# A two-layer decoder on one core: the first layer's decay sums loaded in halves, and its output store moved to the end of the store queue's step

## The reference

```
x = x + state_space(layernorm(x))            # m_ in the kernel
x = x + cross_attention(layernorm(x), ctx)   # c_
x = x + recurrent(layernorm(x))              # r_
```

```
decay = exp(A * dt_t)
state = state * decay + (x_t * dt_t) (outer) B_t
y_t   = state . C_t
y = (y + x * D) * silu(z);  y = y * rsqrt(mean(y*y) + eps) * norm_w
```

```
c = sigmoid(xt.wf + c.uf + bf) * c + sigmoid(xt.wi + c.ui + bi) * tanh(xt.wc + c.uc + bc)
h = tanh(x.wo + c_final.uo + bo)      # for every tile
```

## Time and profile before

| | us |
|---|---|
| median of 3 runs | 3414.84 |
| lowest and highest | 3406.63, 3415.68 |
| the profiled execution | 3411.43 |
| its span | 3409.5 |

### The profile page before, as it was taken

The page is one execution under the profiler, slowest core; times in us unless marked ns, Lnnn a source line. Parts: engine busy times, 40 slices in busy tenths (PEclk is TensorE's granted clock), DMA queues, the critical chain, the costliest instruction groups (busy, mean ns, idle before and its releaser), DMA issues. The chain is left out here.

```text
span 3409.5 us, 95859 instructions
## 1 busy us (share of the span) xinstructions
PE 3084.8 (90%) x27055; PEld 2664.0 (78%) x27056; DVE 2775.2 (81%) x8725; ACT 2260.3 (66%) x8248; POOL 1514.0 (44%) x5113
## 2 busy tenths in 40 slices
PE   6699999999999999999998699989898999499998
PEld 4578888888888888888886577777777777387998
DVE  5588888888888888888885588888888887687776
ACT  4467777777777777777775477777777777143333
POOL 1244444545444544445452155555555554133333
PEclk8789999999999999999999799999999999699999
DMA  6111111111111111111110200000000000023443
GB/s 190 37 36 50 44 41 41 41 48 47 41 41 41 42 47 46 41 41 41 48 48 14 61 20 15 18 15 18 17 17 18 15 19 13 4 103 121 131 136 90
DMA packets 123391, 161.87 MB, mean 47 GB/s; under 512 B 27331, under 2 KB 94832, under 8 KB 123312
## 3 DMA queue, kind: packets, MB, share of 16 engines
q1 hardware_dynamic: 111056, 126.37, 12.7%
q0 software_dynamic: 12256, 34.53, 2.8%
HBM read 102.85 MB, written 61.53 MB: 48 GB/s over the span
## 5 line engine op out<-in xcount | busy, mean ns | idle before, releaser
L380 POOL TENSOR_TENSOR tiny<-tiny 128x1 f32<-128x1 f32 x3456 | 776.0, 225 | 799.1 <-DVE tiny L367 558.3
L806 ACT ACTIVATE work<-bank,att 128x128 f32<-128x128 f32 x2048 | 722.0, 378 | 57.7 <-DVE att L796 51.8
L806 ACT ACTIVATION_READ_ACCUMULATOR work<-bank,att 128x1 f32 x2048 | 445.0, 217 | 0.0
L796 DVE TENSOR_REDUCE att<-bank 128x4 f32<-128x512 f32 x512 | 333.8, 683 | 47.1 <-PE bank L789 47.1
L825 PE MATMUL bank<-const,work 128*128 128x128 f32 x2048 | 318.1, 279 | 31.8 <-ACT work L806 26.1
L789 PEld LDWEIGHTS bank<-work 32*128 32x128 f32 x4096 | 254.0, 189 | 107.0 <-issue 74.7
L1286 DVE SCALAR_TENSOR_TENSOR work<-work,small 128x127 f32<-128x127 f32 (+2 forms) x1152 | 317.5, 345 | 16.0 <-ACT work L1126 10.7
L789 PE MATMUL bank<-work 32*128 32x128 f32 x4096 | 302.7, 286 | 21.1 <-ACT work L1171 2.5
L825 PEld LDWEIGHTS bank<-const,work 128*128 128x128 f32 x2048 | 239.5, 142 | 74.8 <-ACT work L806 58.7
L380 POOL TENSOR_TENSOR tiny<-tiny,const 128x1 f32<-128x1 f32 x1152 | 250.6, 218 | 90.3
L185 PE MATMUL bank<-w1r,workr 128*128 (+2 forms) x802 | 267.5, 333 | 0.5 <-issue 0.2
(11 more groups left out here) (357 smaller groups left out, 8472.8 us busy)
## 6 DMA issues: line engine op xcount, KB each, us to landing
work<-decay_sums SPq DMA_DIRECT2D x64, 512.0 KB, 3.7
work<-pair_rows SPq DMA_DIRECT2D x91, 258.0 KB
pair_rows<-extra SPq DMA_DIRECT2D x128, 182.0 KB
work<-in_ctx SPq DMA_DIRECT2D x128, 128.0 KB, 2.1
x_res<-in_x POOLq DMA_DIRECT2D x8, 1024.0 KB, 17.5
recurrence_out<-r_xo_ SPq DMA_DIRECT2D x64, 128.0 KB, 1.7
work<-recurrence_out SPq DMA_DIRECT2D x64, 128.0 KB
out_dram<-work POOLq DMA_INDIRECT x91, 2.5
```

What stands on the lines that cost most here:

```text
L380: e.tensor_tensor(out_, a_, b_, ALU.add if b_ is three_halves else ALU.mult)\
L796: e.tensor_reduce(a_nm[:, 4 * g:4 * g + 4], sc_banks[g % 2][:, :].rearrange("p (h k) -> p h k", k=P), AX.X, ALU.max, negate=True).then_inc ...
L806: last = e.activation(Pb[g % 2][:, c * P:c * P + P], sc_banks[g % 2][:, c * P:c * P + P], ACT.Exp, bias=a_nm[:, 4 * g + c:4 * g + c + 1], ...
```

## The change

The load of the decay sums becomes two loads of 2 KB per partition, for heads 0 to 3 and 4 to 7, each with a semaphore of its own (`m_cum0`, `m_cum1`). The first waits for the first half of the products of the tile before, the second for the second half. Neither waits for the square, which now writes into `m_zg_` (the gate, which at that point has been used). `m_relative` waits for its own half. In SyncE's step the order becomes: both loads, the context load, the blank stores, and last the output store, which is that of tile i-5 in place of i-4; the pipeline of SyncE runs one step further out.

```diff
-                def load_sums(b):
-
-                    if past(b): e.wait_ge(S["m_y"], 2 * b)
-                    if past(b): e.wait_ge(S["m_ss"], b)
+                def load_sums(b, half):
+
+                    if past(2 * b): e.wait_ge(S["m_y"], 2 * b - 1 + half)
                     src = cum_dram[b] if isinstance(b, int) else cum_dram[ds(b, 1)].rearrange("o n -> (o n)")
-                    e.dma_start(m_E.rearrange("p h t -> p (h t)"), src.partition_broadcast(P))\
-                        .then_inc(S["m_cum"], 16)
+                    at = slice(4 * P * half, 4 * P * half + 4 * P)
+                    e.dma_start(m_E.rearrange("p h t -> p (h t)")[:, at], src[at].partition_broadcast(P))\
+                        .then_inc(S[f"m_cum{half}"], 16)
...
                     if live(b):
-                        load_sums(b)
-                    b = i - 4
-                    if live(b):
-                        store_output(b)
+                        load_sums(b, 0)
+                        load_sums(b, 1)
                     b = i
                     if live(b):
                         load_context(b)
                     b = i
                     if live(b):
                         blank_rows(b)
+                    b = i - 5
+                    if live(b):
+                        store_output(b)
...
-                pipeline(e, 4, step)
+                pipeline(e, 5, step)
...
-                    e.activation(m_E[:, 0:4, :].rearrange("p h t -> p (h t)"), m_y_, ACT.Square, accum_out=m_ss_)\
+                    e.activation(m_zg_, m_y_, ACT.Square, accum_out=m_ss_)\
                         .then_inc(S["m_ss"], 1)
...
-                    e.wait_ge(S["m_cum"], 16 * (b + 1))
+                    e.wait_ge(S[f"m_cum{half}"], 16 * (b + 1))
```

More of the change, by code:

```diff
@@ L101 @@
         m_cur m_xn m_tr m_xnT m_xbc m_raw m_tap m_conv2 m_conv m_z m_ztanh m_zg m_xtanh m_xbcs
-        m_xtr m_g m_xt m_xdt m_xd m_gm m_cum m_rel m_exp m_M m_y m_yx m_y2 m_ss m_seed m_rs
+        m_xtr m_g m_xt m_xdt m_xd m_gm m_cum0 m_cum1 m_rel m_exp m_M m_y m_yx m_y2 m_ss m_seed m_rs
         m_ytr m_yhi m_ylo m_out m_x1 c_stats c_aggr c_seed c_rs c_xn c_ctx c_x1b c_tr c_hi c_lo c_q
```

## The result

| | before | after |
|---|---|---|
| median, us | 3415.26 (4 runs) | 3509.99 (4 runs) |
| lowest and highest | 3406.63, 3416.17 | 3504.18, 3513.74 |
| the profiled execution | 3411.43 | 3504.18 |

The changed kernel is slower by 1.0285 times, 95% interval 1.0271 to 1.0299. The two profiled executions are 92.8 us apart.

What follows compares the result with a forecast made beforehand. TensorE, busy 25.81 of 26.97 us a period, was taken to set the pace. -25 us (load stall) and +94 us (store wait) gave +69 on 3411.4: 3480, named as 3482 for the median; range 3440 to 3535.

Steps and rivals of the forecast that it cites:

- the forecast +69: Whole kernel: -25 us from the load stall plus 94 us from the store wait; 70% chance, within 3455 to 3510.
- The delay of 1.60 us: TensorE idling before `c_project`, as line 1196 awaits the output store: 1.60 us a period, 59 times, +94 us.
- the 4.22 us: SyncE's own issuing between the context load's issue and the output store's, behind the blanks: 4.22 us.
- The landing of 1.7 us: Output store behind the blanks: from issue to landing 1.7 us, shortest and median of 64 stores.
- The gain of 0.41 us: VectorE's wait for the decay sums goes; line 1119, then bound by `m_project`, starts 0.41 us sooner a period, -25 us.
- The first, the store in time: Rival (a): line 1196 isn't held, only the load stall's gain is left: -25 us, 3388; 9%.
- The threshold at 2.76 us: Rival (a) holds if the store is issued 2.76 us behind the end of `c_transpose`; the rows give 4.40.
- The second, the late landing behind the blanks: Rival (b): output store lands 3.1 us after issue, costing 3.0 us a period: +152, 3563; 8%.
- the prediction's 3.1: Longest landing of 64 output stores, 3.1 us, taken by rival (b) for the store behind the blanks.
- The third, the whole stall of 1 us coming back: Rival (c): the decay sums' load stall is gained back whole, 62 x 1.0 us: +32 us, 3446; 9%.
- The rest: The square's new place, one more DMA issue a step on SyncE, and the earlier context load: 0 each.

Runs made afterwards that it cites:

- The last run: Changed kernel with the output store right behind the two loads, and VectorE's `m_residual` moved behind the second `m_relative`: 3395.4 us against 3407.0 before, ratio 0.9961.

## Why the prediction was right, and where it was off

The direction and the mechanism were right: slower, since the store of tile i-5 can't be issued before `c_transpose` of the period in which line 1196 needs it landed, and `c_project` on TensorE waits for what stands behind. The waits predicted for the profile are there, 59 of them at line 1197. But the measured +94.7 us (92.8 between the profiled executions) lie well above the forecast +69, and two terms of the sum came out smaller than said, by 0.34 and 0.31 us a period. That their errors cancel is luck. A third term was missing.

| term | predicted | measured |
|---|---|---|
| delay of `c_project`, a period | 1.60 | 6.60 - 5.34 = 1.26 |
| gain at the decay sums, a period | 0.41 | 26.79 - 26.69 = 0.10 |
| net, a period | about 1.2 | 28.00 - 26.79 = 1.21 |
| falls of TensorE's clock | 0 | 14 x 1.4 = 20 us |

59 x 1.21 and the 20 us of the clock make 91 of the 92.8 us between the two profiled executions. The two single terms give 1.16 and not 1.21; the 0.05 between is not explained.

- **The delay of 1.60 us** was too large, mainly by the issuing. I took the 4.22 us from the context load to the load of the sums in the earlier trace rows for the distance to the store; it is 3.90. In the earlier trace rows the issue of the load follows the end of the last blank's by 0.59 us; the store's follows it by 0.27 (1041.20 + 0.89 to 1042.36). So the distance between two issues depends on which DMA comes next, not only on how many stand ahead; the load stands at the head of SyncE's next step, behind two waits, and which part of this makes the difference is not shown. The landing of 1.7 us, read from the earlier trace rows, held. The reading of the earlier trace rows as DMA engines standing still did not quite: those rows lie 0.93 us behind the end of the last blank's issue, the store goes out 0.27 us behind it, and at that time the share is still 0.63 (1042.3 to 1042.4). But the data of the large blanks are through at 1042.7, before the store's begin to move at 1043.2.
- **The gain of 0.41 us** failed twice. It was worked out from one period with a wait of 1.19 us, and the mean of the earlier trace rows is 0.96. And `m_project` does lead line 1120, as foretold (it ends 0.04 us before it in the kernel with the store behind the loads, 1010.46 and 1010.50), but it is not the next to be late. That is GpSimd's Newton steps: VectorE's `m_residual` waits 0.77 us for them, the maxima behind it end after the taps, and the convolution starts on the maxima. The last run shows this: with that covered, another 0.12 us a period come out, 26.79 - 26.57 = 0.22 in all. So of the 0.31 us that the term was too large, 0.12 are the Newton steps, and the rest is, as far as the runs tell, the one period. I had named only TensorE as the next bound, and had not followed VectorE's own list with the wait taken out.
- **The clock** is the step that is missing. The prediction says that TensorE idles 1.60 us a period and takes this for the whole price. The run with the gap filled shows that the idling itself costs another 14 to 20 us: the clock falls behind some of the gaps. The earlier trace rows held no warning, since no gap in the loop of before was as long: TensorE's longest wait in its table of 300 to 1780 us is 0.7 us, or 0.9 with its weight loads.
- **The rivals.** The first, the store in time, is what two of the runs have, with 5 us of gain and not 25. The threshold at 2.76 us behind the end of `c_transpose` that it names was worked out with a landing of 1.7 us. It doesn't hold close to the blanks: issued at 2.97 us (2.80 behind the context load, itself 0.17 behind `c_transpose`), the store brought a wait of 0.84 us. The second, the late landing behind the blanks, didn't happen in the changed kernel, but did as soon as the store stood closer to the large ones; it is their data, still moving on one DMA engine, and adds 0.5 to 0.8 us and not the 1.4 of the prediction's 3.1. The third, the whole stall of 1 us coming back, was refuted by 0.10 us.
- **The rest** was free as predicted: the square's place (ratio 1.0002), the second DMA issue, the earlier context load.

## What to carry to other kernels

A DMA that frees a buffer is part of a loop: before moving it in an in-order queue, write down for every wait ahead of it in which period that wait ends, and compare the landing with the next writing of the buffer. The period in which data are ready says nothing, if a wait for the next period stands ahead. And a stall that is taken away is worth only the distance to the next thing that is late on each engine's own list; follow all of them, from a typical period and not from one.

## What the runs showed of the hardware that was not expected

- TensorE's granted clock fell from 2.4 to 1.2 GHz behind gaps of about 1.1 us in 14 of 57 periods (15 in another execution), and stayed low for about 3 us; behind gaps of 2.2 us it did in 50 of 57, behind gaps of 0.76 us in none. Each of the 14 falls made its period 1.3 to 1.5 us longer. The Trainium skill ("TensorE: Matmul & The Clock Gate", A second HAM failure mode: psum-queue depth-cycling) tells of a kernel in which short idling between groups of products makes the clock go up and down; the trace here agrees, and filling the gap with repeated products took the falls away and 14 us of the time.
- The same 128 KB store to DRAM lands 1.7 us after its issue when no large transfer is left ahead of it, 2.2 us right behind one blank store of 182 KB, 2.5 us behind two, and a median 3.0 us right behind the two loads of the sums. The last costs nothing, for its buffer is needed 25 us later. In the first three cases ScalarE goes on some 0.4 us behind the end of the data. In the second and third the last data move at 20 to 30 GB/s and a share of 0.06 to 0.09, as if on one DMA engine in 16, for 0.2 to 0.5 us after the others are done; a share in slices of half a microsecond hides this.
